# A decoder block on one core: the weighted values of the layer stage in one phase of 32 products instead of two phases of 16, with the output laid out by sequence

## What is computed

```python
def attn_layer(x, Wqkv, qs, ksc, Wo):
    qkv = x @ Wqkv                       # 16 heads of 64
    ...
    q = l2norm(q) * qs;  k = l2norm(k) * ksc
    q = q * cos * scale + rotate_half(q) * sin * scale
    k = k * cos * inv + rotate_half(k) * sin * inv
    out = local_attention(q, k, v)       # banded softmax inside a sequence
    out = out.transpose(0, 2, 1, 3).reshape(b, n, INNER)
    return out @ Wo
for i in range(DEPTH):
    x = attn_layer(shift_tokens(x), Wqkv[i], q_scale[i], k_scale[i], Wo[i]) + x
    x = ffn_layer(shift_tokens(x), ...) + x
```

## Time and profile before

| | |
|---|---|
| median of 3 runs | 4349.85 us (4349.69 to 4352.57) |
| profiled execution, its span | 4352.3 us |
| TensorE busy | 4168.5 us (96%) |
| VectorE busy | 3653.6 us (84%) |
| ScalarE busy | 3390.6 us (78%) |
| GpSimd busy | 2644.6 us (61%) |
| layer stage, roughly | from 560 to 3460 us of the span |

### The profile page before, as it was taken

How to read it: one execution, slowest core, us unless ns; L and a number is a source line. 1 busy time by engine, 2 the same in 40 slices (tenths; PEclk the granted TensorE clock), 3 DMA queues, 4 the chain that set the end, 5 groups by cost and what they waited for, 6 DMA issues and landing times.

```text
span 4352.3 us, 150350 instructions
## 1 busy us (share of the span) xinstructions
PE 4168.5 (96%) x61520; PEld 3088.7 (71%) x61520; DVE 3653.6 (84%) x11101; ACT 3390.6 (78%) x9585; POOL 2644.6 (61%) x2210
## 2 busy tenths in 40 slices
PE   7999989999999999999999999999999889999999
PEld 5777756666666666666666666666666578888888
DVE  4665689999999999999999999999999566776765
ACT  3545478989999899989999899989999556666665
POOL 3444477777777777777777777777777333333331
PEclk9888799999999999999999999999999889999999
DMA  3000000000000000000000000000000100000000
GB/s 103 4 4 4 5 2 4 4 4 4 29 4 3 4 29 4 4 4 4 29 4 4 4 29 3 4 4 9 26 7 7 33 2 4 4 4 4 4 4 6
DMA packets 65256, 46.40 MB, mean 11 GB/s; under 512 B 29220, under 2 KB 63032, under 8 KB 63800
## 3 DMA queue, kind: packets, MB, share of 16 engines
q1 hardware_dynamic: 64568, 36.78, 3.0%
HBM read 28.48 MB, written 2.10 MB: 7 GB/s over the span
## 4 chain that ended last, share of the span: by engine, by line
PE 77%; DVE 12%; ACT 8%; issue 2%; POOL 1%; SPq 0%; DMA 0%; DVEq 0%; POOLq 0%; ACTq 0%
PE ps L564 63%; PE ps L568 14%; DVE BIG L1126 5%; ACT BIG L907 4%; ACT BIG L915 3%; DVE sm L1137 3%; DVE BIG L1134 1%; POOL BIG L1587 1%; DVE BIG L1131 1%; ACT ps L907 1%; DVE sm L1134 0%; DVE BIG L1204 0%; DVE BIG L1130 0%; DVE rs L1126 0%; DVE x_sb L1126 0%
## 5 line engine op out<-in xcount | busy, mean ns | idle before, releaser
L564 PE MATMUL ps<-WB,BIG 128*128 128x128 f32 (+2 forms) x8576 | 1988.2, 366 | 48.0 <-DVE BIG L1134 41.0
L907 ACT ACTIVATE BIG<-ps 128x512 f32<-128x512 f32 (+5 forms) x3168 | 1446.8, 514 | 535.5 <-PE ps L568 347.2
L1587 POOL TENSOR_TENSOR BIG<-BIG,sm 128x512 f32<-128x512 f32 (+1 forms) x864 | 1223.0, 1425 | 720.0 <-DVE sm L1338 536.6
L564 PEld LDWEIGHTS ps<-WB,BIG 128*128 128x128 f32 (+1 forms) x8576 | 1132.6, 192 | 274.9 <-issue 151.3
L1587 POOL TENSOR_TENSOR BIG<-BIG 128x512 f32<-128x512 f32 x768 | 966.4, 1278 | 93.1 <-DVE BIG L1126 92.8
L568 PEld LDWEIGHTS ps<-t_ident,BIG 128*128 128x128 f32 x6016 | 726.6, 146 | 353.4 <-issue 251.0
L564 PEld LDWEIGHTS ps<-BIG 64*64 64x64 f32 (+2 forms) x37888 | 648.8, 131 | 458.9 <-issue 273.5
L568 PE MATMUL ps<-t_ident,BIG 128*128 128x128 f32 x6016 | 911.9, 283 | 53.6 <-DVE BIG L1126 24.0
L1137 DVE TENSOR_REDUCE sm<-BIG 128x8 f32<-128x512 f32 (+3 forms) x1472 | 879.8, 613 | 37.8 <-ACT BIG L915 35.1
L564 PE MATMUL ps<-BIG 64*64 64x64 f32 (+4 forms) x37888 | 812.2, 227 | 64.5 <-ACT BIG L907 19.4
L1590 POOL TENSOR_TENSOR sm<-sm,halfn 128x1 f32<-128x1 f32 (+2 forms) x336 | 290.5, 871 | 744.7 <-DVE sm L1130 410.2
(11 more groups left out here) (121 smaller groups left out, 3027.8 us busy)
## 6 DMA issues: line engine op xcount, KB each, us to landing
WB<-in_Wqkv SPq DMA_DIRECT2D x6, 1536.0 KB, 6.9
XS<-y_sb SPq DMA_DIRECT2D x96, 63.0 KB
y_sb<-in_ctx SPq DMA_DIRECT2D x16, 256.0 KB, 3.2
WB<-in_Wo SPq DMA_DIRECT2D x6, 512.0 KB, 8.1
x_sb<-in_x SPq DMA_DIRECT2D x8, 256.0 KB, 5.1
WB<-in_F_W SPq DMA_DIRECT2D x1, 2048.0 KB, 9.1
WB<-in_F_W SPq DMA_DIRECT2D x8, 256.0 KB, 5.0
out<-x_sb SPq DMA_DIRECT2D x8, 256.0 KB, 2.3
```

The lines of the kernel that those rows point to most:

```text
L564: return te.matmul(o, l, r, start=start, stop=stop, skip_group_check=not check)
L907: return se.activation(o, i, ACT.Copy)
L1587: return pe_.tensor_tensor(o, a, b, op)
```

## The change

Phase w is gone. Phase y does all 32 products at the place that w had, after q1. It runs over the halves, the heads, and then the two sequences. Bank y{b} now holds sequence b of both halves, so it is written by one row half of the array only. ScalarE's o0 and o1 wait for y and copy one sequence each, into the k buffers of both halves (64 columns of every 128). PE's o therefore waits for both copies before its first product. The waits of ScalarE's v, a and b for w of the unit three tiles earlier become waits for y. The bank turns follow the new order of the list: q1 takes its bank ahead of y0 and y1 instead of behind them.

```diff
 C_ORDER = {
-    "pe": "1b06 1a06 2g26 2a26 1v06 1b16 2a18 2g16 1a16 1y8 1q14 1w8 1k04 1x3 1v15 2tr5 1s6 1p07 2g07 1k14 1o8 1p17 "
-           "2o8 2a07 1q03",
+    "pe": "1b06 1a06 2g26 2a26 1v06 1b16 2a18 2g16 1a16 1q14 1y8 1k04 1x3 1v15 2tr5 1s6 1p07 2g07 1k14 1o8 1p17 "
+          "2o8 2a07 1q03",
...
+        def c_OT(u):
+
+            n = 2 * (NT * u.at["l"] + u.at["t"]) % 6
+            two = BIG[:, 10240 + 2048 * n:14336 + 2048 * n].rearrange("p (f c) -> p f c", f=2)
+            return two[:, :, 512:1024].rearrange("p f (g c) -> p f g c", c=128)
...
-            elif u.kind == "C2" or ph != "w":
+            else:
                 take(u, ph, EMPTIED[u.kind[1] + ph], 1, 6)
...
-                elif ph in "yw":
+                elif ph == "y":
 
                     for m in ("p0", "v0", "p1", "v1"):
                         w.wait_ge(*u.on("act", m))
-                    if ph == "w":
-                        w.wait_ge(*u.on("pe", "y"))
-                    for i in range(8):
-                        hp, par = i // 2, i % 2
-                        for hf in range(2):
-                            b, K, bb = c_bufs(u, hf), bank[u.bank[f"y{hf}"]], (hf + (ph == "w")) % 2
-                            q, r = slice(64 * bb, 64 * bb + 64), half(hf, par)
-                            o = mm(K[64 * par:64 * par + 64, 256 * bb + 64 * hp:256 * bb + 64 * hp + 64],
-                                   b.VV[q, 64 * i:64 * i + 64], b.PT[q, 128 * hp + r.start:128 * hp + r.stop])
+                    for hf in range(2):
+                        b = c_bufs(u, hf)
+                        for i in range(8):
+                            hp, par = i // 2, i % 2
+                            c, r = 256 * hf + 64 * hp, 128 * hp + half(hf, par).start
+                            for bb in range(2):
+                                q = slice(64 * bb, 64 * bb + 64)
+                                o = mm(bank[u.bank[f"y{bb}"]][64 * par:64 * par + 64, c:c + 64],
+                                       b.VV[q, 64 * i:64 * i + 64], b.PT[q, r:r + 64])
                     o.then_inc(u.name("pe", ph, sems), 1)
                 elif ph == "o":
+                    w.wait_ge(*u.on("act", "o0"))
+                    w.wait_ge(*u.on("act", "o1"))
                     for hf in range(2):
-                        w.wait_ge(*u.on("act", f"o{hf}"))
                         b = c_bufs(u, hf)
...
                 elif ph[0] == "v":
                     w.wait_ge(*u.on("pe", ph))
                     if three:
-                        w.wait_ge(*three.on("pe", "w"))
+                        w.wait_ge(*three.on("pe", "y"))
...
                 elif ph[0] == "o":
-                    w.wait_ge(*u.on("pe", "w"))
-                    o = copy(b.OT.rearrange("p (g b i) -> p b g i", b=2, i=64), K.rearrange("p (b g i) -> p b g i", b=2, i=64))
+                    w.wait_ge(*u.on("pe", "y"))
+                    o = copy(c_OT(u)[:, :, :, 64 * int(h):64 * int(h) + 64], K.rearrange("p (f g i) -> p f g i", f=2, i=64))
```

## The result

| | before | after |
|---|---|---|
| median | 4349.69 us (4346.08 to 4352.57, 5 runs) | 4370.53 us (4360.40 to 4379.59, 5 runs) |
| profiled execution: time, span | span 4352.3 us | 4364.36 us, span 4362.5 us |
| TensorE busy | 4168.5 us | 4117.2 us |
| a regular round of the layer stage | 58.76 us | 59.40 us |

The ratio is 1.0047, with a 95% interval of 1.0032 to 1.0061: the change makes the kernel slower, by 0.5%. The forecast was 4366 us.

A forecast was written before the change was run, and what follows sets the result against it. PE was taken as the bound before; a new wait through ACT and DVE then sets rounds: +16.8 (layers 2 to 6) +2.4 (first layer) -2.4 (layer ends) -0.5 (stage start, end) = +16.3, giving 4366 us; range 4345 to 4386.

The forecast's parts named there:

- The saving on PE: Layer stage: the joined block takes 1.09 us, saving 0.35 or 0.32 us a unit, 66 us in all, 1.37 a round.
- the sign: Named beforehand as showing the forecast right: PE's busy time down by some 60 us, with the span up.
- The new wait and the path: Once a round p0(77) waits for DVE's q1(80); the ring through ACT, DVE and PE makes rounds 59.24 us, 0.48 longer.
- The sum: Whole kernel: regular rounds, first layer, layer ends, and start and end of the stage add up to +16.3 us.
- The 35 rounds inside layers 2 to 6: Seven rounds in each of these layers, 0.48 us longer each: +16.8 us.
- The first layer, with the start of the stage: First layer's six rounds at 0.4 us each: +2.4; the stage's start shared a separate -0.5 with its end.
- Four layer ends: PE's stall for DVE's q0 shortens and the clock may stay up: -0.6 us each, -2.4 together, bounds -0.2 and -1.9 each.
- End of the stage: Layer stage's end, forecast together with its start: -0.5 us, between -3 and +1.
- All of the gain (1): p0(77) doesn't wait for DVE's q1(80), or it is ready in time: 4284 us; chance 0.13, part gains included.
- Nothing to measure (2): Layer ends give back 1.9 us each and the first layer adds nothing, or DVE's path is shorter: +6, 4356 us; chance 0.14.
- The clock at the new stall (3): PE's stall at p0(77) lets the clock fall each round, 1.6 us a time: +66 more, 4432 us; chance 0.06.
- The joined block as slow as y and w adjoining (4): Array halves hinder each other, so the block takes 1.4 us or more: rounds of 59.6, 4380 us; chance 0.04.

The follow-up runs named there:

- the first run: Changed kernel with the joined phase kept in place, but the six banks' turns as in the kernel before: 4335.19 us, ratio 0.9944.
- the second run: Kernel before with phases y and w untouched, only q1 given its bank ahead of y0 and y1, as in the change: 4385.15 us, ratio 1.0068.
- the third: Changed kernel with the joined phase moved ahead of q1, the place of the former first phase: 4337.74 us, ratio 0.9953.
- the eighth run: Changed kernel with the joined phase ahead of q1 and, in ACT's list, gelu g1 ahead of the square of q1: 4325.14 us, ratio 0.9949.

## Why the prediction was right

**The saving on PE**: right. The block takes the 1.09 us taken from the scores. PE's work fell, by the starts, by 1.4 us a round. Its busy time fell by 51 us, where some 60 had been named as the sign.

**The new wait and the path**: right, and shown from both sides: take the turns away and the stall and the loss go; put the turns alone into the kernel before and the round grows to 59.70 us. In the changed kernel the path measures 1.06 + 19.08 + 13.83 + 0.05 + 25.38 = 59.40 us (from the trace's unrounded times; the rows above give some terms 0.01 off); the forecast was 1.06 + 19.05 + 13.81 + 0.05 + 25.27 = 59.24. Of the missing 0.16, 0.06 lies in PE's restart behind the stall (p0 to k1 takes 0.50 us instead of 0.44), 0.05 ahead of the joined phase of unit 77, which starts that much later behind q1(81) than the others do, and 0.05 in ACT's and DVE's stretches. I had priced the release of a wait, and not that the group behind it takes longer.

**The sum**, by PE's starts in the profiled execution. The 35 rounds inside layers 2 to 6: +22.2 us, forecast 16.8, for the 0.16 above. The first layer, with the start of the stage: +2.9, forecast 2.4. Four layer ends: -6.3, forecast -2.4 with a bound of -7.6. End of the stage: +1.8, where start and end had -0.5 together, outside the bound of +1; I had no row for it and didn't follow it up. Together +20.6, forecast +16.3. The rounds came out 5.4 us above their term and the layer ends 3.9 below theirs, and these two errors offset each other in part: that the median of 4370.5 lies so near the forecast 4366 is partly luck.

The layer ends gave back more because the clock mostly kept up. PE's timeline at the end of layer 2 of the changed kernel, beside the earlier trace rows:

```profile
1472.51 2.08 PE L570 MATMUL ps<-WB,BIG 128*128 128x512 f32 x2 [2.25 <-DVE BIG L1133]
```

PE's timeline at the end of layer 3:

```profile
1951.69 1.13 PE L570 MATMUL ps<-WB,BIG 128*128 128x512 f32 x2 [2.24 <-DVE BIG L1133]
```

The table by stretches around both, with the clock:

```profile
1470.00:1482.00 12.00, 9.75 (x150) 5.64 (x149) 9.18 (x27) 6.26 (x14) 7.06 (x5) 0.86 0.01 1
1946.00:1958.00 12.00, 9.76 (x158) 5.82 (x158) 10.63 (x27) 8.07 (x16) 8.36 (x7) 1.00 0.01 1
```

The stall is 2.25 us instead of 3.14. At the first end the clock fell to 1.2 GHz all the same, and that end gained 0.1 us; at the three others it stayed at 2.4 GHz, and they gained 1.5 to 3.0. The 3.0 is at the last of them, where before the change the clock had been low for 6.8 us and not for 3.4 as at the other ends. I had the mechanism as a bound and took a third of it.

**Span against median.** The span grew by 10.2 us and the median by 20.8. The text ahead takes the span of 4352.3 us for the profiled execution's own time, but in every run recorded with both the span is 1.8 to 1.9 us below the time. By that its time was about 4354.2 us (an estimate), 4.5 above the median of five, while the profiled execution of the changed kernel, 4364.36 us, lies 6.2 below its own: that is the difference. The forecast, a sum of steps, doesn't rest on it.

In the profiles the layer stage takes 20.6 us longer (PE starts on it 6.0 us earlier than in the profile before and ends 14.6 us later), and the stages behind it, which the change doesn't touch, take 4.4 us less. In those stages and ahead of the layer stage the clock goes up and down: its mean is 0.85 in the first 560 us and 0.96 from 3460 to 4300 us, in both profiles. From run to run the mean clock and the time move together (0.976 with 4360.40 us, 0.968 with 4379.59). So the agreement of the medians with the layer stage's +20.6 is partly chance; the rounds are the firmer evidence.

**The rivals.** All of the gain (1): wrong, for the reason given. Nothing to measure (2): the layer ends gave back nearly what it supposed, but the rounds grew by a third more than forecast. The clock at the new stall (3): it stayed at 1.00 in regular rounds. The joined block as slow as y and w adjoining (4): it takes 1.09 us. The rule of the Trainium skill, Perfetto Trace Analysis, section Identifying the Most-Contended Engine, to optimize the engine of highest occupancy first, would have held only with the old turns, and then for a quarter of PE's saving (58.76 to 58.44 us, of a possible 57.4). The same section says that for TensorE the busy time of the matmuls is no good measure of the headroom, and that the busy time of the weight loads is one; in the round of the earlier trace rows these loads (PEld) are busy for 39.77 of 58.76 us, less than DVE's 55.73, so this measure would not have put TensorE first.

## What to carry to other kernels

When buffers are given out in turn along an engine's order, moving one phase past another changes who waits for whom far from the edit: list for each phase near it whose bank it takes, before and after, and when that is emptied. If an engine at 99% has another at 95% beside it, follow the chain of every near wait back until it reaches the full engine again; the sum around that ring is the least that the new round can be, and it can be added up from rows before anything is built. It is the new round only if no other ring is longer; the runs above met several that were near. Before moving an instruction ahead of another, ask who waits for the one that is moved back, and count again what lies on the path.

## What the runs showed of the hardware

A stall costs PE more than its length: behind the stall ahead of p0(77), the four transposes took 0.50 us to the next start instead of 0.44; in the first run q1(80), behind its stall, took 1.06 instead of 0.95. And idle stretches of one length don't settle the clock: after 2.25 us it fell at one layer end and held at three, in the same execution, and in the first run the same idle time let it fall at two ends and hold at two. At these layer ends it held after every stall of 1.64 us (the second run) and fell after every one of 3.14 us and more (the kernel before, the third and the eighth run).
